# Two of the four key-weight loads issued from ScalarE's DMA queue instead of the sync engine's

## The reference

```python
x   = x + xattn(layernorm(x), ctx, ctx, mask)       # x, ctx: 8 x 256 x 512
x   = x + ffn(layernorm(x))
# xattn: 16 heads of 32; q, k, v = in @ W.T + b
k_prime = relu(k @ Wkf.T) * mask                     # 64 features a head
kv      = einsum('bhnf,bhne->bhfe', k_prime, v)
out     = (relu(q @ Wqf.T) @ kv) / (q' @ sum(k_prime) + 1e-8) @ Wo.T + bo
# ffn: bit_linear(x, w) = activation_quant(x) @ weight_quant(w).T   (8-bit rows, ternary weights)
activated = subln(up * relu(gate)**2)                # 2048 wide
y         = bit_linear(activated, w_down)
```

## Time and profile before

| | us |
|---|---|
| median of 3 runs | 427.86 (427.54 to 429.09) |
| the profiled execution: its own time | 430.05 |
| the profiled execution: its span | 428.0 |
| PE busy | 414.2 (97%) |
| PEld busy | 282.6 (66%) |
| DVE busy | 341.2 (80%) |
| ACT busy | 287.0 (67%) |
| POOL busy | 145.4 (34%) |

### The profile page before, as it was taken

The page is one execution under the profiler, slowest core; times in us unless marked ns, Lnnn a source line. Parts: engine busy times, 40 slices in busy tenths (PEclk is TensorE's granted clock), DMA queues, the critical chain, the costliest instruction groups (busy, mean ns, idle before and its releaser), DMA issues.

```text
span 428.0 us, 11266 instructions
## 1 busy us (share of the span) xinstructions
PE 414.2 (97%) x4835; PEld 282.6 (66%) x4835; DVE 341.2 (80%) x505; ACT 287.0 (67%) x406; POOL 145.4 (34%) x290
## 2 busy tenths in 40 slices
PE   7989999997999999999999999999999999999995
PEld 5889889986878855844764575575467566464443
DVE  4544849566939949998987897999998898998983
ACT  5674989892145277779539647764883978939970
POOL 0000000002433732384281545536225533444660
DMA  7992656543202010023313033031303121423055
GB/s 219 416 415 87 233 214 214 233 156 144 101 5 87 38 26 2 12 51 87 71 40 64 0 87 74 14 74 40 64 31 61 34 49 21 84 71 65 11 121 150
DMA packets 51170, 42.42 MB, mean 99 GB/s; under 512 B 43056, under 2 KB 44080, under 8 KB 49200
## 3 DMA queue, kind: packets, MB, share of 16 engines
q1 hardware_dynamic: 51120, 41.70, 32.3%
HBM read 27.01 MB, written 4.19 MB: 73 GB/s over the span
## 4 chain that ended last, share of the span: by engine, by line
PE 58%; DVE 17%; ACT 8%; POOL 6%; issue 5%; DMA 5%; SPq 0%; DVEq 0%; POOLq 0%; ACTq 0%
PE ps L353 48%; DVE zb L359 3%; DVE rows_of L365 3%; PE ps L561 2%; PE ps L683 2%; POOL tk L362 2%; PE ps L588 2%; ACT rb L356 2%; DMA xs<-in_wu_dram 2%; PE ps L660 2%; DVE tk L767 2%; ACT kT L356 2%; POOL zb L359 1%; DMA xqT<-xqb 1%; PE ps L622 1%
## 5 line engine op out<-in xcount | busy, mean ns | idle before, releaser
L353 PE MATMUL ps<-tg,xqT 128*128 128x512 bf16 x256 | 60.6, 380 | 0.8 <-DMA xqT<-xqb 0.7
L353 PE MATMUL ps<-tu,xqT 128*128 128x512 bf16 x256 | 60.6, 379 | 0.2 <-DVE zb L359 0.2
L362 POOL TENSOR_SCALAR tk<-tk 128x1 f32<-128x1 f32 x96 | 39.4, 411 | 36.9 <-DVE tk L718 19.4
L353 PE MATMUL ps<-td,yqT 128*128 128x512 bf16 x208 | 46.9, 379 | 0.0
L353 PEld LDWEIGHTS ps<-tu,xqT 128*128 128x128 bf16 x256 | 24.3, 98 | 31.1 <-issue 2.1
L356 ACT ACTIVATE rb<-zb 128x1024 f32<-128x1024 f32 x29 | 30.6, 1055 | 21.0 <-DVE zb L359 20.9
L353 PEld LDWEIGHTS ps<-tg,xqT 128*128 128x128 bf16 x256 | 23.5, 98 | 30.8 <-issue 2.5
L359 DVE TENSOR_TENSOR zb<-ps,rb 128x1024 f32<-128x1024 f32 x29 | 35.3, 1217 | 6.8 <-ACT rb L356 6.7
L353 PE MATMUL ps<-aph,wkh 128*128 128x256 f32 x128 | 36.2, 287 | 1.5 <-DVE wkl L359 0.6
L353 PE MATMUL ps<-aph,wqh 128*128 128x256 f32 x128 | 37.1, 290 | 0.0
L767 DVE TENSOR_REDUCE tk<-zb 128x1 f32<-128x1024 f32 x30 | 36.2, 1207 | 1.1 <-POOL zb L359 0.8
(11 more groups left out here) (134 smaller groups left out, 1052.2 us busy)
## 6 DMA issues: line engine op xcount, KB each, us to landing
xs<-in_wg_dram SPq DMA_DIRECT2D x4, 1024.0 KB, 13.1
xs<-in_wu_dram SPq DMA_DIRECT2D x4, 1024.0 KB, 6.2
xs<-in_wd_dram SPq DMA_DIRECT2D x4, 1024.0 KB, 7.8
xs<-in_x_dram SPq DMA_DIRECT2D x8, 512.0 KB, 4.5
out_dram<-xs SPq DMA_DIRECT2D x15, 256.0 KB, 2.1
craw<-in_ctx_dram SPq DMA_DIRECT2D x7, 512.0 KB, 7.5
xs<-in_wk_dram SPq DMA_DIRECT2D x4, 256.0 KB, 4.7
xs<-in_wv_dram SPq DMA_DIRECT2D x4, 256.0 KB, 6.8
```

The source lines that it names most:

```text
L353: return add("pe", name, cost, waits, lambda e: e.matmul(out, lhsT, rhs, start=start, stop=stop))
L362: return add(lane, name, cost, waits, lambda e: e.tensor_scalar(out, a, s1, s2, op0, op1))
```

## The change

The load helper gets a lane, and `Wk.in0` and `Wk.in1` are put into lane `act`: ScalarE's queue issues them, in the place that the planner gives them among ScalarE's own instructions. The other loads stay on `sp`. The 2.9 us per MB and the 0.47 us for an issue are the planner's for both lanes.

```diff
-        def dma(name, mb, waits, out, in_, sem):
+        def dma(name, mb, waits, out, in_, sem, lane="sp"):
             if sem not in dma_names:
                 dma_names.append(sem)
-            return add("sp", name, 2.9 * mb, waits, lambda e: e.dma_start(out, in_), sem)
+            return add(lane, name, 2.9 * mb, waits, lambda e: e.dma_start(out, in_), sem)
...
         def load_piece(c):
-            dma(f"Wk.in{c}", 0.25, [], slot[0][:, cw[c]], wk_d[:, cw[c]], f"Wk{c}")
+
+            dma(f"Wk.in{c}", 0.25, [], slot[0][:, cw[c]], wk_d[:, cw[c]], f"Wk{c}", "act" if c < 2 else "sp")
```

## The result

| | before | changed |
|---|---|---|
| median of 22 runs each, us | 428.70 | 428.87 |
| lowest, highest | 427.44, 429.65 | 427.81, 431.07 |
| ratio to before, 95% interval | | 1.0023 (1.0013 to 1.0033) |
| the profiled execution: own time, span | 430.05, 428.0 | 428.8, 426.8 |

By the ratio, whose interval leaves out 1, the change makes the kernel slower by 0.23%, about 1.0 us (0.6 to 1.4). The sign is clearer than the size. The two medians are only 0.17 us apart, because the runs of before fall into two groups (ten from 427.4 to 428.1, twelve from 428.7 to 429.7) and their median stands at the edge of the upper one; the means, 428.47 and 429.20, are 0.73 apart. The one profiled execution of the changed kernel has a shorter span than the one before; why a single pair of spans can't judge this change is part of what follows.

A forecast was written before the change was run, and what follows sets the result against it. TensorE, busy 414.2 of 428.0 us, was taken as the bound. Piece 1 late by 1.3 us, with table and remaining order at 0, gave 427.86 + 1.3 = 429.2 us, range 427.1 to 431.0.

The forecast's parts named there:

- The order: ScalarE's list at the start: first weight copy falls behind `ctx0.hi2`, `Wk.hi1` behind `Wk.hi2`; VectorE's order follows.
- Its cost: TensorE's key piece 1 starts at 9.57 instead of 8.28, 1.29 us late; ends 0.6 and 2.0.
- the landing of `Wk.in2`: Load of a key weight piece at the start: little gain from earlier issue, landing at 7.6 instead of 7.86.
- Nothing gives time back: Whole kernel: TensorE is full, so a delay at the start isn't made good; loss at 8.28 counts in full.
- the 1.1 us: TensorE's idle time between the warm matmuls and 8.28: the most an earlier load can win, 0.26% of the time.
- Rival 1: TensorE's clock falls in the longer gap before piece 1, 1.3 us on top of the forecast: 430.5; chance 0.15.
- The table: `table` moves behind `Wv.hi3`; a second load of 1.28 us near 13.7 costs nothing, without cover up to 1.5.
- Rival 2: A later stage, where loads and TensorE's results race, or the tail, is worse ordered: 1.5 us more, 430.7; chance 0.15.
- Rival 3: Loads win at the start: `Wk.in2` lands before 6.32, TensorE gains 0.5 to 1.1 us: 427.0; chance 0.10.
- Rival 4: Nothing to see: early issue is worth the lost place, time within 0.3 of 427.9; chance 0.10.

The follow-up runs named there:

- e1: Changed kernel's order of ScalarE and VectorE, but all loads back on SP in the old order; 431.08 us, 1.0018 of before.
- e2: Kernel before with the two loads at the head of ScalarE's queue, every engine's order otherwise as before; 428.96 us, 0.9978 of before.
- e6: Changed kernel with ScalarE's lane free at 0.0 instead of 1.9 in the planner; 429.39 us, 0.9977 of before.
- e4: Changed kernel with the step table put back ahead of ctx0.hi0, behind the two loads; 430.38 us, 1.0026 of before.
- e9: Changed kernel with 14 extra matmuls of 8 columns behind the last warm one; 427.70 us, 0.9965 of before.
- e8: Kernel before with two more VectorE memsets that hold the warm matmuls back, no TensorE instruction added; 431.05 us, 1.0031 of before.
- the control: The kernel before itself, run and profiled again, nothing changed; 430.25 us, 1.0016 of its own runs.
- e7: Kernel before with 14 extra matmuls of 8 columns behind the last warm one; 427.11 us, 0.9936 of before.
- e10: Changed kernel with ScalarE's lane free at 0.0 in the planner and 14 extra 8-column matmuls; 426.68 us, 0.9933 of before.
- e11: Kernel before with 14 extra 8-column matmuls, run again on another chip comparison; 427.65 us, 0.9961 of before.

## Why the prediction was right

**The order** was predicted step by step and came out so; the lists of the two programs differ in nothing more than the steps named, the swap of `ctx2.hi0` and one more of VectorE's (`Wq.lo1` ahead of `v0.1.rows`), and from 25 us on they are the same. e1 and e2 show that the order is the cause of the late piece 1 in the first trace; in the second one it was the landings and the clock.

**Its cost** was put at 1.29 us, with ends of 0.6 and 2.0. Measured: 1.77 in the first trace, 1.49 in e1. The mis-sized term is the landing of `Wk.in2`: 2.12 + 6.0 = 8.1 us instead of the 7.6 assumed, and later than the 7.86 of before despite the earlier issue. It lies inside the bounds that the prediction gave, near the upper one, 8.36. The size is not a fixed one: with the same issues `Wk.in2` landed at 8.03 in e6, 8.51 in e4 and 7.52 in e9. The Trainium skill, "DMA: Bandwidth & Descriptors", section "Issuing engines are not separate DMA queues", says that the DMAs of both queues run on the same DMA engines and interleave. The trace agrees: what `Wk.in0` won by 0.8 us, `ctx0.in0` lost by 1.2. From the second copy of the pair at 8.12, which starts at 8.64, it took 1.41 us to TensorE's start at 10.05, against 1.42 from the earlier trace rows.

**"Nothing gives time back" was wrong**, and it hid the mis-sized term: 1.3 forecast and 1.0 measured lie so near each other in part by luck, a delay put too low and a give-back put at nothing. The step read the earlier trace rows as showing no slack and took the wait at 101 for a fixed sum; the stretch from 10 to 40 us, with 1.48 us idle, was not among the windows on which it rested. e8 shows the give-back in its time, 1.3 us for more than 3 at the start. Where the changed kernel gets it back isn't shown: the waits at 21 and 27 us differ between the two traces of before by as much, and the wait at 101 was shorter in the two traces of the changed kernel but not in e1 and e4. For the same reason the 1.1 us that the prediction took as the most to be won is the idle time of one trace; the control's trace has none there.

**Rival 1, the clock**, was taken as an addition with a chance of 0.15, on the ground that after 1.84 us idle at 101 the clock had held. That row was one draw of a coin: the same wait lowered it in the control. It also fell in the gap that the change opens, in two of four traces. It is part of the measured 1.0 us, not a case by itself: of the 0.73 us between the means of the first comparison 0.37 are left without the four runs of the changed kernel that had a lowered clock (430.81 us on average). On the second chip the runs at full clock are 0.5 us apart (429.69 and 429.17) and those with a lowered one 2.2 (433.06 and 430.89); they are no more frequent there in the changed kernel, 5 of 12 against 13 of 29.

**The table** cost nothing, as said: e4. **Rival 2**, a later stage worse ordered, didn't come: the lists are the same from 25 us on, and the traces show no new wait of TensorE over 1 us. **Rival 3** is out, since `Wk.in2` landed at 8.1 and 6.3 would have been needed. **Rival 4**, within 0.3 us of no change, is out by the ratio and its interval, though not by the two medians.

**Still open:** why TensorE waits at 21, 27, 101 and 142 us. The profile names no releaser. That it goes with the place in TensorE's own list rests on e7, where 14 more matmuls at the head of the list took the wait at 101 away with all else in place, on the two waits that moved by exactly 14, and on the fact that the wait at 101 comes back at the same matmul (behind 107 of 128 of a `kv` block) in both traces of before and in both of the changed kernel. How the instructions come to the engine was not itself tried. And whether the early issue gains when the weight copies keep their turn isn't settled over all pairs: e2, e6 and e10 against e11 all came out about 1 us faster, but each alone stands little above the 0.16% by which the control missed itself, and e2's trace shows no earlier features that would say where the gain arises.

## What to carry to other kernels

A load moved to another engine's queue is also moved in every list that a planner makes from that engine's free time: follow the order through before pricing the issue, because an in-order engine that copies piece after piece turns one swapped pair into a wait for the later landing. An earlier issue on a second queue can be paid by the landing of its neighbour, as here, where one won 0.8 us and the other lost 1.2. Before a change of 1 us is judged by two traces, look for waits of the bound engine that nothing releases: they vary by as much from run to run, and a second trace of the kernel against itself gives the size that can be told.

## What the runs showed that I had not expected

- Fourteen matmuls of 8 columns (0.5 us in the trace) ahead of a 430 us kernel made it 0.4 to 0.6% faster (0.9936 and 0.9961). A wait of TensorE of 1.84 us was gone, and two others stood exactly 14 matmuls earlier.
- Behind an idle time of 1.76 to 1.91 us of TensorE its granted clock went to 0.50 in some executions and not in others, and one of 2.32 us left it at full; matmuls of 256 columns then started 0.21 us apart instead of 0.11. The 17 of 35 runs of before with a lowered clock took 1.5 us longer than the rest.
- With two loads of 256 KB moved to a second queue, the first 128 KB of the other queue landed in 3.2 to 5.1 us in the seven traces, and in 2.3 to 2.7 us in the seven with one queue, though issued at the same moment. Two queues made that landing later and also less regular.
- The profile gives TensorE's clock as 1.00 while the warm matmuls of 512 columns start 0.43 us apart, the pace of the lower level as the control shows it at 103 us (PEclk 0.50). At the start the distance between matmuls tells the level, and the clock column doesn't.
